# First turns of each token tile written out, bias products in another PSUM bank, and products dealt six and two, then four and four

## What is computed

```python
# x: (512, 128) after attention; flat_x = layernorm(x)
current = zeros(T)
for _ in range(8):                       # levels 0..7 of a binary tree, 255 nodes
    score = einsum('td,td->t', flat_x, w1s[current]) + b1s[current]
    current = current * 2 + choice(score) + 1
path_weights = gelu(abs(logits))
for i in range(8):
    t_i = einsum('td,tdo->to', flat_x, w2s[nodes_i]) + b2s[nodes_i]
    out = out + t_i * path_weights[:, i][:, None]
return x + out
```

## Time and profile before

| what | value |
|---|---|
| median of 3 runs | 131.72 us (130.14 to 132.13) |
| the profiled execution's own time | 130.12 us |
| its span in the trace | 128.4 us |
| mean granted TensorE clock | 0.97 of full speed |
| busy share of the span | TensorE 83%, VectorE 73%, ScalarE 54%, GpSimd 30% |

### The profile page before, as it was taken

One profiled execution on the slowest core, in us unless ns is written; L12 is line 12 of the kernel. 1 busy time (PEld: TensorE's weight loads), 2 busy tenths in 40 slices (PEclk: granted clock), 3 DMA queues, 4 the chain that ended last, 5 costly groups with the idle time before them and its releaser, 6 DMA issues.

```text
span 128.4 us, 3400 instructions
## 1 busy us (share of the span) xinstructions
PE 106.4 (83%) x980; PEld 77.2 (60%) x981; DVE 93.6 (73%) x296; ACT 68.8 (54%) x160; POOL 38.1 (30%) x67
## 2 busy tenths in 40 slices
PE   6899799649999999998899569989898988997910
PEld 2259464317656656575748236488687977977900
DVE  2789799989688979982588898655466475757480
ACT  4047368645696797792119388356433535543510
POOL 6393000000000000000040000355479659885623
PEclk9999999995999999999999999999999999999995
DMA  3996799998998000002989000030002002020000
GB/s 82 329 314 198 332 490 419 393 482 378 439 475 347 36 3 0 5 0 80 372 367 455 20 0 0 0 84 2 23 3 28 0 0 20 0 23 0 0 0 20
DMA packets 3662, 19.97 MB, mean 156 GB/s; under 512 B 417, under 2 KB 2336, under 8 KB 3136
## 3 DMA queue, kind: packets, MB, share of 16 engines
q1 hardware_dynamic: 2576, 18.68, 36.1%
q0 software_dynamic: 496, 0.33, 2.1%
q10 hardware_dynamic: 576, 0.79, 2.0%
HBM read 19.27 MB, written 0.52 MB: 154 GB/s over the span
## 4 chain that ended last, share of the span: by engine, by line
PE 39%; DVE 17%; issue 8%; DVEq 8%; ACT 6%; POOL 1%
PE turn_ps L751 10%; PE s_ps L907 6%; DVE early L1213 6%; DVEq L92 5%; PE s_ps L697 4%; PE turn_ps L907 2%; ACT prob L528 2%; PE misc_ps L716 2%; PE aux_ps L716 2%; PE turn_ps L926 2%; DVE token_path L1119 2%; DVEq L97 2%; PE s_ps L784 1%; PE s_ps L636 1%; ACT prob_t L524 1%
## 5 line engine op out<-in xcount | busy, mean ns | idle before, releaser
L528 ACT ACTIVATE prob<-prob,negmax 128x512 f32<-128x512 f32 x32 | 21.7, 716 | 5.5 <-DVE negmax L1079 5.5
L1079 DVE CUSTOM_DVE_ANT_0 prob<-s_ps,mask 128x512 f32<-128x512 f32 x32 | 21.0, 686 | 3.3 <-PE s_ps L697 2.6
L751 PE MATMUL turn_ps<-ident,prob 128*128 128x128 f32 x128 | 20.1, 294 | 3.4 <-ACT prob L528 3.4
L437 POOL TENSOR_TENSOR early<-early,scaled_sb 128x256 f32<-128x256 f32 x24 | 19.1, 796 | 11.5 <-ACT scaled_sb L608 9.6
L1213 DVE SCALAR_TENSOR_TENSOR early<-s_ps,coef,early 128x128 f32<-128x128 f32 x40 | 12.2, 347 | 13.5 <-issue 6.3
L907 PE MATMUL s_ps<-w,msg 128*128 x128 | 18.5, 287 | 2.9 <-issue 1.6
L751 PEld LDWEIGHTS turn_ps<-ident,prob 128*128 128x128 f32 x128 | 14.6, 147 | 10.2 <-ACT prob L528 8.9
L907 PEld LDWEIGHTS s_ps<-w,msg 128*128 128x128 f32 x128 | 15.5, 191 | 5.8 <-issue 5.7
L403 POOL TENSOR_TENSOR rstd<-veps,mhalf 128x2 f32<-128x2 f32 x2 | 1.4, 714 | 54.0 <-DVE veps L950 54.0
L608 ACT ACTIVATE scaled_sb<-s_ps,coef 128x128 f32<-128x128 f32 x24 | 8.8, 368 | 11.2 <-PE s_ps L907 11.1
L907 PE MATMUL turn_ps<-w,msg 128*128 x64 | 9.8, 275 | 0.0
(11 more groups left out here) (204 smaller groups left out, 201.8 us busy)
## 6 DMA issues: line engine op xcount, KB each, us to landing
w<-in_w_t SPq DMA_DIRECT2D x3, 4096.0 KB, 22.9
w<-in_w_t SPq DMA_DIRECT2D x1, 4032.0 KB, 13.5
w<-in_adj SPq DMA_DIRECT2D x1, 1024.0 KB, 9.0
w_sb<-in_w_t ACTq DMA_DIRECT2D x1, 384.0 KB, 4.7
x_sb<-in_x SPq DMA_DIRECT2D x1, 256.0 KB, 3.0
msg<-in_neigh_t SPq DMA_DIRECT2D x1, 256.0 KB, 4.5
out_x<-x SPq DMA_DIRECT2D x1, 256.0 KB, 3.8
row_sb<-in_rows ACTq DMA_DIRECT2D x1, 255.5 KB, 7.4
```

Source lines behind the costliest of these rows:

```text
L437: nc.gpsimd.tensor_tensor(mine, mine, scaled_sb[:, slots[0]:slots[-1] + 1, :], ALU.add).then_inc(pooled[i], TURN)
L528: nc.scalar.activation(prob[:, u % RING, :], prob[:, u % RING, :], ACT.Exp, bias=negmax[:, t, h:h + 1], scale=-1.0).then_inc(exped, 1)
L751: last = nc.tensor.transpose(turn_ps[u % 2][:, m * P:(m + 1) * P], prob[:, u % RING, m * P:(m + 1) * P], ident[:])
L1079: nc.vector.tensor_tensor_reduce(out=prob[:, u % RING, :], in0=score_ps[u % RING], in1=mask[:, t, :], scale=1.0, scalar=0.5 * MASKED, op0= ...
```

## The change

It writes out the first turn of every tile (with constant list addresses), so that each tile's loop holds the turns from the second on and runs at least once: all lists are turned up to at least 32 entries. In these written-out turns VectorE and GpSimd do the end of the tile before after half 0 of the new tile's first turn (`late=True`) instead of ahead of it; TensorE and ScalarE do it ahead, as before. The deal is turned round: VectorE has six banks of half 0 and four of half 1, ScalarE two and four. Loads of entries are of 4 or 8 registers. The bias products go to bank 1. The last tile's sums are added up in another order, with the last product's sum last.

```diff
--- before.py
+++ after.py
@@ -35,13 +35,14 @@
 STEP = 2 * HALF
 HALVES = 2
 TURN = HALVES * STEP
-DVE_BANKS = ((0, 2, 5, 7), (0, 2, 3, 4, 5, 7))
-ACT_BANKS = ((1, 3, 4, 6), (1, 6))
+DVE_BANKS = ((0, 2, 3, 4, 5, 7), (0, 2, 5, 7))
+ACT_BANKS = ((1, 6), (1, 3, 4, 6))
 DVE_SUMS = 3
+GROUP = 4
 POOL_SUMS = 2
 SUMS = DVE_SUMS + POOL_SUMS
 LISTED_AT = [[(d + a).index(j) for j in range(STEP)] for d, a in zip(DVE_BANKS, ACT_BANKS)]
-BIAS_BANK = 4
+BIAS_BANK = 1
 BIASED_AFTER = ((0, 2), (2, 4))
 TURNED_IN = (1, 4)
 DVE_ORDER = [(half, j) for half in range(HALVES) for j in DVE_BANKS[half]]
@@ -111,26 +112,29 @@
 def list_lengths(nc, engine, entries):
 
     _, lengths = nc.values_load_multi_w_load_instructions(
-        entries[0:1, 0:TILES], engines=(engine,), min_val=TURN, max_val=NODES_PAD,
-        skip_runtime_bounds_check_because="lengths are counts of nodes turned up to at least one turn")
+        entries[0:1, 0:TILES], engines=(engine,), min_val=2 * TURN, max_val=NODES_PAD,
+        skip_runtime_bounds_check_because="lengths are counts of nodes turned up to at least two turns")
     return lengths
 
 
-def tile_turns(eng, lengths, turn, begun, after):
-
-    def whole_turn(s, e, at):
+def tile_turns(eng, lengths, turn, begun, after, late=False):
+
+    start = end = STEP
+    for s in range(TILES):
+        if s > 0 and not late:
+            after(s - 1, end)
         for half in range(HALVES):
-            turn(s, half, e + half * STEP, at + half * STEP)
-
-    start = STEP
-    whole_turn(0, STEP, 0)
-    begun()
-    for s in range(TILES):
+            turn(s, half, start + half * STEP, s * NODES_PAD + half * STEP)
+            if s > 0 and late and half == 0:
+                after(s - 1, end)
+        if s == 0:
+            begun()
         end = eng.snap((lengths[s] & (2 * NODES_PAD - TURN)) + start)
-        with eng.Fori(start + TURN if s == 0 else start, end, TURN) as e:
-            whole_turn(s, e, e - start + s * NODES_PAD)
-        after(s, end)
+        with eng.Fori(start + TURN, end, TURN) as e:
+            for half in range(HALVES):
+                turn(s, half, e + half * STEP, e - start + s * NODES_PAD + half * STEP)
         start = end
+    after(TILES - 1, end)
 
 
 def gnn_ffn_kernel(nc, x, adj, neigh_t, w_t, cols, rows, w1_t, w2_t, b2, out):
@@ -423,6 +427,8 @@
                                              ).then_inc(read_back, 16)
 
             def add_scaled(s, half, e, at):
+                if isinstance(at, int) and half == 0 and 1 <= s <= len(BIASED_AFTER):
+                    pool.wait_ge(bias_moved, s)
                 for i, slots in enumerate(SLOTS_ADDED):
                     if ACT_ORDER[slots[-1]][0] != half:
                         continue
@@ -441,8 +447,6 @@
 
                 if s < TILES - 1:
                     pool.wait_ge(pooled[-1], end + STEP)
-                    if s == 0:
-                        pool.wait_ge(read_back, 16)
                     nc.gpsimd.tensor_tensor(result[:, s, :], acc[:, DVE_SUMS, s, :], acc[:, DVE_SUMS + 1, s, :], ALU.add
                                             ).then_inc(result_ready, 1)
                     pool.wait_ge(result_ready, 2 * s + 1)
@@ -464,7 +468,7 @@
                     nc.gpsimd.indirect_dma_start(out=out, out_offset=bass.IndirectOffsetOnAxis(
                         ap=token_s[:, s:s + 1], axis=0), in_=result[:, s, :], in_offset=None).then_inc(stored, 16)
 
-            tile_turns(nc.gpsimd, lengths, add_scaled, read_last, store)
+            tile_turns(nc.gpsimd, lengths, add_scaled, read_last, store, late=True)
             pool.wait_ge(stored, 16 * TILES)
 
         @block.scalar
@@ -598,7 +602,7 @@
             entry = entry_registers(nc.scalar, "entry_act", STEP)
 
             def scale(s, half, e, at):
-                own_entries(nc, nc.scalar, entry[0:len(ACT_BANKS[half])], nodes, at, len(DVE_BANKS[half]))
+                own_entries(nc, nc.scalar, entry[0:GROUP], nodes, at, GROUP)
                 if isinstance(e, int) and half == 0:
                     act.wait_ge(coef_ready, 2)
                 for i, j in enumerate(ACT_BANKS[half]):
@@ -606,7 +610,7 @@
                     slot = ACT_ORDER.index((half, j))
                     act.wait_ge(pooled[slot // POOL_SUMS], e + (1 - half) * STEP)
                     nc.scalar.activation(scaled_sb[:, slot, :], product_ps[j], ACT.Copy,
-                                         scale=coef[:, s, bass.ds(node_at(nc.scalar, entry, i), 1)]
+                                         scale=coef[:, s, bass.ds(node_at(nc.scalar, entry, len(DVE_BANKS[half]) - GROUP + i), 1)]
                                          ).then_inc(emptied[j], STEP)
 
             def move_turned():
@@ -902,7 +906,7 @@
                         pe.wait_ge(weights_added, 1)
                     if s == 0 and not isinstance(e, int) and half == 0 and j in TURNED_IN:
                         pe.wait_ge(coef_t_ready, 1 + TURNED_IN.index(j))
-                    if half == 0 and j == BIAS_BANK and 1 <= s <= len(BIASED_AFTER):
+                    if half == 0 and j == BIAS_BANK and 1 <= s <= len(BIASED_AFTER) and isinstance(at, int):
                         pe.wait_ge(bias_moved, s)
                     nc.tensor.matmul(product_ps[j], hs_t[:, s * P:(s + 1) * P],
                                      w2_flat[:, bass.ds(found[LISTED_AT[half][j]], D)], start=True, stop=True
@@ -1170,9 +1174,7 @@
                     choose(1, GROUPS[1][0] + i)
                     dve.wait_ge(picked_split, 2 * i + 2)
             length = misc_ps[0:1, 2 * TILES:3 * TILES]
-            nc.vector.tensor_scalar(turned_up[:, 0:1], length[:, 0:1], TURN - 1.0, 2.0 * TURN, ALU.add, ALU.max)
-            then(nc.vector.tensor_scalar(turned_up[:, 1:TILES], length[:, 1:TILES], TURN - 1.0, float(TURN),
-                                         ALU.add, ALU.max))
+            then(nc.vector.tensor_scalar(turned_up[:], length, TURN - 1.0, 2.0 * TURN, ALU.add, ALU.max))
             nc.vector.tensor_scalar(entries[:], turned_up[:], -TURN, None, ALU.bitwise_and).then_inc(lengths_ready, 1)
             nc.vector.memset(coef[:, :, NODES:NODES_PAD], 0.0)
 
@@ -1196,9 +1198,11 @@
             entry = entry_registers(nc.vector, "entry_dve", STEP)
 
             def add_up(s, half, e, at):
-                own_entries(nc, nc.vector, entry[0:len(DVE_BANKS[half])], nodes, at, 0)
+                own_entries(nc, nc.vector, entry[0:-(-len(DVE_BANKS[half]) // GROUP) * GROUP], nodes, at, 0)
                 if isinstance(e, int) and half == 0:
                     dve.wait_ge(coef_ready, 2)
+                if isinstance(at, int) and half == 0 and s == READ_BACK:
+                    dve.wait_ge(read_back, 16)
                 for i, j in enumerate(DVE_BANKS[half]):
                     at_turn = DVE_ORDER.index((half, j))
                     slot = at_turn % DVE_SUMS
@@ -1215,21 +1219,23 @@
                         in1=mine, op0=ALU.mult, op1=ALU.add).then_inc(emptied[j], STEP)
 
             def sum_up(s, end):
-                for _, j in DVE_ORDER[-DVE_SUMS:]:
-                    dve.wait_ge(emptied[j], end)
-                nc.vector.tensor_reduce(dve_sum[:, s, :], acc[:, 0:DVE_SUMS, s, :].rearrange("p j d -> p d j"),
-                                        AX_X, ALU.add).then_inc(halved, 1)
                 if s < TILES - 1:
-                    if s + 1 == READ_BACK:
-                        dve.wait_ge(read_back, 16)
+                    for _, j in DVE_ORDER[-DVE_SUMS:]:
+                        dve.wait_ge(emptied[j], end)
+                    nc.vector.tensor_reduce(dve_sum[:, s, :], acc[:, 0:DVE_SUMS, s, :].rearrange("p j d -> p d j"),
+                                            AX_X, ALU.add).then_inc(halved, 1)
                 else:
+                    for _, j in DVE_ORDER[-DVE_SUMS:-1]:
+                        dve.wait_ge(emptied[j], end)
                     dve.wait_ge(pooled[-1], end + STEP)
-                    dve.wait_ge(halved, TILES)
-                    then(nc.vector.tensor_tensor(dve_sum[:, s, :], dve_sum[:, s, :], acc[:, DVE_SUMS, s, :], ALU.add))
-                    nc.vector.tensor_tensor(result[:, s, :], dve_sum[:, s, :], acc[:, DVE_SUMS + 1, s, :], ALU.add
+                    mine = acc[:, 1:DVE_SUMS, s, :]
+                    then(nc.vector.tensor_tensor(mine, mine, acc[:, DVE_SUMS:SUMS, s, :], ALU.add))
+                    then(nc.vector.tensor_tensor(dve_sum[:, s, :], acc[:, 1, s, :], acc[:, 2, s, :], ALU.add))
+                    dve.wait_ge(emptied[DVE_ORDER[-1][1]], end)
+                    nc.vector.tensor_tensor(result[:, s, :], dve_sum[:, s, :], acc[:, 0, s, :], ALU.add
                                             ).then_inc(tile_done, 1)
 
-            tile_turns(nc.vector, lengths, add_up, lambda: None, sum_up)
+            tile_turns(nc.vector, lengths, add_up, lambda: None, sum_up, late=True)
 
 
 _INS = ("x", "adj", "neigh_t", "w_t", "cols", "rows", "w1_t", "w2_t", "b2")
```

## The result

| | before | after |
|---|---|---|
| median of 20 runs | 131.50 us | 132.11 us |
| ratio (runs of like clock) | | 1.0142 [1.0106, 1.0178] |
| profiled execution: own time, span | 130.12, 128.4 us | 132.83, 131.0 us |
| stage of products, first to last product | 39.66 us | 41.06 us |
| last product's end to the result | 2.54 us | 2.62 us |

The change costs 1.4%, 1.9 us, where 3.9 us was forecast; 132.11 lies under the range of 133.3 to 137.4. The medians differ less than the ratio, which leaves out the slow runs, 11 of the 20 of the kernel before and 6 of the 20 of after. In both traces TensorE is granted half its clock for some microseconds at about 30 us: over the window 28:36 the granted clock is 0.79 in the trace of before and 0.63 in that of after, and the stage starts at 82.73 and 83.93.

The account below looks back on a forecast made before the run. No engine alone was taken to set the pace: TensorE had the largest share, VectorE 25%. Terms 4.36 - 1.2 + 0.9 - 0.7 + 0.4 + 0.1 = +3.9 us gave 135.5 us, range 133.3 to 137.4.

Parts of the forecast that it names:

- the tail: From the last product's end to the result: 2.62 us instead of 2.54, so +0.1.
- the biases' bank: Bias products moved from bank 4 to 1: -1.2 for waits ahead of them, +0.9 for waiting on the copy behind them.
- the deal and the loads: Turned deal and loads of 4 and 8: VectorE stops falling behind in turns 3, 5 and 7, -0.7.
- the late ends: VectorE's reduce behind half 0 makes TensorE wait from tile 2 to 3, +0.4; GpSimd's late store costs nothing.
- The added turn: Tile 2 gets a second turn, all coefficients zero, making nine turns for eight: +4.36.
- TensorE's own way out of a loop: Ahead of the bias products, what is late once the waits for VectorE go: some 0.1 each time.
- The wait for the copy: Second product of the half behind the bias products waits 0.48 and 0.42 for the biases' copy: +0.9.
- They spare no gap: Written-out turns spare TensorE no gap but the one between tiles 2 and 3, and a loop is entered instead: 0.
- the limit of 1.5: TensorE may run some 1.5 us ahead of VectorE's first product of a half before it waits.
- TensorE at its own pace: Rival, chance 0.13: shorter loads and written-out heads free TensorE of all gaps, nine turns of 4.16: +1.2, 132.9 us.
- point of decision: Average turn of 4.30, bank 1 waits included, decides for the pace rival; the forecast's own average is 4.44.
- The two others: Rivals: late reduce and store back up TensorE, +5.3, 137.0 us, chance 0.21; no turn added, -0.5, 131.2 us, chance 0.04.

Follow-up runs that it names:

- after_again: The changed kernel profiled a second time with no edit: stage 41.56 us, ratio 1.011 to the kernel before.
- loads_only: The kernel before with register loads of 4 and 8 instead of 4, 6 and 2, nothing else: stage 38.70 us, ratio 0.996.
- old_deal: The changed kernel with the old deal of banks (VectorE four then six, ScalarE four then two): stage 42.14 us, ratio 1.015.
- looped_old_deal: The changed kernel with the old deal and no written-out turns, keeping the ninth turn, bank 1, loads and new tail: stage 41.85 us, ratio 1.016.
- ends_ahead: The changed kernel with VectorE and GpSimd doing a tile's end ahead of the next tile's written-out turn: stage 41.17 us, ratio 1.006.
- five_taken: The changed kernel with VectorE leaving out its bank 3 product in every half 0: stage 41.56 us, ratio 1.014.

## Why the prediction was wrong

The stage, from before to after_again: 39.66 + 4.38 (turn) - 1.21 (bank) - 0.96 (loads) - 0.31 (written-out turns, deal and late ends together) = 41.56, +1.90. The last term is what is left over, and no larger than chance. The prediction had +3.8 in the stage, +0.1 in the tail. So it was 1.9 too high: 0.9 of it in the biases' bank (-0.3 forecast, -1.21 measured), 1.0 in the other parts but the turn (-0.7 for the deal and the loads and +0.4 for the late ends make -0.3, measured -0.96 and -0.31).

- The added turn: right. Two turns between the second and the third reduce, and +4.38 for 4.36. That the change is slower hangs on this alone.
- The biases' bank: the step that failed first. The prediction gave -1.2 and +0.9; the one constant measures -2.0 and +0.7, -1.21 net with 0.1 in the other turns. Two terms were mis-sized. I charged 0.1 for TensorE's own way out of a loop, and there is no wait at all (93.05). And I took 2.08 as a half's pace without gaps, and that figure, too, holds a gap: eight products take 1.88 (91.83 to 93.71 above). What the other 0.2 is differs from half to half. In turns 6 and 8 it was VectorE and ScalarE, since their shorter loads alone take it away (loads_only). At 90.44, TensorE's own load of the next entries can be it: it began at 89.6, 0.84 ahead. No experiment shows that. The bias products themselves took 0.1 less each time, for which I had no term. The wait for the copy was sized right (0.48 and 0.42 forecast, 0.49 and 0.43 seen), but not what it costs: each time the half that is held up gives 0.1 of it back.
- The new deal and the loads: I gave them -0.7 together. The loads alone measure -0.96, the deal alone nothing certain (-0.6 in one pair of kernels, +0.8 in another). So the term was nearly of the right size, and that is luck: VectorE's falling behind in turns 3, 5 and 7, which was its reason, is not where the loads gain. The two fours at 0.69, taken as 0.67, are 0.60.
- "They spare no gap": the second step that failed. In the new deal the written-out heads save 1.1 us in all, 1.5 with the ends ahead. Tile 3's head takes 3.78 for 4.36. Each entry into a loop saves 0.4 to 0.5 (half 1 of turns 3, 5 and 7 in old_deal against looped_old_deal), where I had written that a loop is entered instead: 0. In these kernels entering a loop is cheaper than jumping back. The loop turns behind the heads give it back in part, and with the old deal in full. For turn 4 the late ends are the reason (4.29 to 3.85 with them ahead), for turns 6 and 8 it is open. These sizes come from single profiles.
- The late ends: the sum is right by luck (+0.4 forecast, 0.4 measured), the place is wrong. VectorE's reduce is hidden at every head. At tile 3's, where I feared for it, VectorE was not near the limit of 1.5 before but past it (1.97), which is the wait of 0.41 at 115.96; in the changed kernel it is 0.97 there (113.66 behind 112.69). GpSimd's store, which I costed at nothing, holds up ScalarE. Its buffers are wanted in the turn after, as the prediction says, but GpSimd is then still 1.5 us behind.
- The tail: right to 0.01, with two misses of 0.1 that cancel.

Of the rivals, "TensorE at its own pace" came nearest: it gave +1.2, and the turns average (41.56 - 1.5 - 2.0) / 9 = 4.23, where its own point of decision was 4.30; that is also the sign by which the prediction was to be wrong. The two others fall: there are nine turns, and no wait of TensorE for VectorE shows in the stage. The reason of the one that came nearest holds in part. TensorE keeps 1.88 in four of nine halves 0, and loses 0.7 behind each of the loop turns 6 and 8. Why these two are so long stays open. ScalarE's wait for GpSimd isn't the cause, since ends_ahead has 0.6 us of it instead of 4.3 and keeps gaps of 0.71 and 0.69. The deal has a part in it, since old_deal has 0.33 and 0.31 there; by which engine is not shown. For VectorE's last item of half 0 there is only the hint in five_taken.

The load of registers: the trace of after bears out the reading against the rule of 200 ns per register in the Trainium skill, "Runtime: NRT & Kernel Launch", section "Instruction fetch mechanics". Eight registers took 607 ns, 76 each.

## What to carry to other kernels

Before taking a repeated stretch's shortest time for an engine's own pace, look inside it for the piece without any hand-over (here eight products in a row, 1.88 us, against 2.08 from half to half); a floor read too high hides the gain of every edit that removes small gaps. Test a bundle part by part, and in pairs: of this one, a constant and a rounding of load sizes gave 2.2 us of stage, the two parts that took the most code gave 0.3 (no more than chance), and the least list length that they brought with them cost 4.4. And when work is moved behind something, look for who waits for the engine that does it, one turn later.

## What the runs showed of the hardware that I had not expected

- Of the register loads in these stages, fours and eights were quicker than what leaves two over: VectorE 0.34 for 4, 0.81 for 6, 0.60 for 8; ScalarE 0.31 for 4, 0.49 for 2 (single ones took up to 0.3 longer). Loading two unused registers beside six was quicker than loading the six.
- TensorE's own load of 8 entries (0.59) was hidden where it began 0.85 us ahead of the next half: at 99.5 in the changed kernel, with the next half at 100.35 and no gap. Where it began at 98.2 in the kernel before, the next half started at 98.98, 0.54 later than in a row without a gap (98.44, a product's 0.22 behind the last at 98.22). Where between the two it begins to show was not measured.
- The hint for a loop's closing branch cost 3 us of stage in its one profile, with one stall of 2.46 us on VectorE; its four runs took 133.32 to 137.34.
- The same program's first stretch differs by 0.4 us from one profile to the next (4.97 and 5.35), with a register load on TensorE of 0.60 in the one and 0.84 in the other.
